# Moving three ScalarE, GpSimd and VectorE steps within a batch round of a cross-attention and routed feed-forward kernel

## The reference

```python
# attention with 8 heads of 64 channels; q = layernorm(x), k = v = context
ig, fg = gates(concat(q, k, v))                       # 8 rows of 512 each
csum   = cumsum(log_sigmoid(fg))
log_D  = where(tril, csum_i - csum_j + ig_j, -inf)
D      = exp(log_D - max(log_D))                      # the decay
C      = (q @ k.T / 8 + q . rpe[hops]) * D
h      = C / (max(abs(sum(C)), exp(-max_log_D)) + 1e-6) @ v
x      = x + layernorm_per_head(h) * (1 + ln_w) + ln_b
# feed-forward: a dense layer, and a mixture of the best two of 10 experts (2 of them null), rank 16
y      = layernorm(x)
w      = top2(softmax(y @ gate_w.T))
x      = x + y @ base_w.T + base_b + 2 * sum_e w_e * (y @ A_e.T) @ B_e.T
```

## Time and profile before

| | us |
|---|---|
| median of 3 runs (4051.57 to 4079.62) | 4066.55 |
| the profiled execution's own time | 4108.5 |
| its span, first to last instruction | 4106.8 |
| PE busy | 3321.3 (81%) |
| DVE busy | 2492.5 (61%) |
| POOL busy | 2075.7 (51%) |
| ACT busy | 1915.9 (47%) |

### The profile page before, as it was taken

One profiled execution on the slowest core, in us unless ns is written; L12 is line 12 of the kernel. 1 busy time (PEld: TensorE's weight loads), 2 busy tenths in 40 slices (PEclk: granted clock), 3 DMA queues, 4 the chain that ended last, 5 costly groups with the idle time before them and its releaser, 6 DMA issues.

```text
span 4106.8 us, 70340 instructions
## 1 busy us (share of the span) xinstructions
PE 3321.3 (81%) x24884; PEld 2008.6 (49%) x24884; DVE 2492.5 (61%) x5113; ACT 1915.9 (47%) x4609; POOL 2075.7 (51%) x2248
## 2 busy tenths in 40 slices
PE   5665667767667766666799999999999999999998
PEld 3433434434444434443455555555555555555554
DVE  4333433334433443434688887878788787878885
ACT  1323323323333333333566566666656565566654
POOL 4555455554555555554345454544545454545544
PEclk7788888787888888888899999999999999999999
DMA  6777777777787778787555555555545555555542
GB/s 195 249 233 223 247 235 225 246 244 233 247 253 249 247 246 258 246 260 238 169 164 174 161 166 161 171 163 166 168 154 173 156 166 156 167 159 176 161 139 83
DMA packets 409680, 814.15 MB, mean 198 GB/s; under 512 B 100314, under 2 KB 204762, under 8 KB 407284
## 3 DMA queue, kind: packets, MB, share of 16 engines
q1 hardware_dynamic: 303860, 453.05, 35.4%
q0 software_dynamic: 87040, 285.28, 23.3%
q10 hardware_dynamic: 18432, 71.31, 4.6%
HBM read 632.67 MB, written 176.69 MB: 197 GB/s over the span
## 4 chain that ended last, share of the span: by engine, by line
PE 52%; DVE 12%; issue 8%; another core or an unknown queue 7%; DMA 6%; SPq 6%; POOL 5%; ACT 5%; ACTq 0%; POOLq 0%; DVEq 0%
PE psum L1445 15%; PE psum L1461 10%; SPq L562 5%; PE psum L1558 5%; PE psum L1528 5%; PE psum L1607 4%; PE psum L1540 4%; DMA arena<-gate_rows 3%; PE psum L1472 3%; PE psum L1611 2%; PE psum L1415 2%; DMA gate_rows<-arena 2%; DVE arena L498 2%; PE psum L1587 2%
## 5 line engine op out<-in xcount | busy, mean ns | idle before, releaser
L674 POOL DMA_INDIRECT arena<-in_L_xattn_rpe_dram,arena x768 | 730.1, 951 | 559.1 <-PE psum L1445 251.8
L1445 PE MATMUL psum<-arena 128*128 128x128 f32 x4352 | 744.9, 322 | 271.4 <-DVE arena L489 89.0
L1445 PEld LDWEIGHTS psum<-arena 128*128 128x128 f32 x4352 | 579.3, 165 | 562.6 <-issue 425.5
L498 DVE COPY arena<-psum 128x416 f32<-128x416 f32 (+15 forms) x512 | 224.1, 441 | 831.7 <-remote 356.4
L1461 PE MATMUL psum<-arena 64*32 64x416 f32 (+7 forms) x8192 | 513.1, 480 | 232.8 <-ACT arena L489 70.7
L498 ACT COPY arena<-psum 128x416 f32<-128x416 f32 (+15 forms) x512 | 199.3, 390 | 888.7 <-remote 361.4
L857 ACT ACTIVATE arena<-arena 128x512 f32<-128x512 f32 (+3 forms) x1024 | 497.7, 557 | 143.2 <-DMA arena<-gate_rows 103.3
L1607 PE MATMUL psum<-arena 128*128 128x512 f32 x1024 | 497.0, 599 | 23.2 <-DVE arena L1158 21.6
L1198 DVE TENSOR_TENSOR arena<-psum,arena 128x1024 f32<-128x1024 f32 (+1 forms) x384 | 387.2, 1043 | 152.1 <-PE psum L1540 147.0
L665 POOL DMA_INDIRECT arena<-in_L_xattn_rpe_dram,arena x320 | 302.7, 946 | 331.7 <-PE psum L1445 207.7
L693 POOL TENSOR_SCALAR_AFFINE_SELECT arena<-arena 128x256 f32<-128x256 f32 x256 | 139.8, 546 | 493.9 <-ACT arena L857 492.8
(11 more groups left out here) (106 smaller groups left out, 4879.5 us busy)
## 6 DMA issues: line engine op xcount, KB each, us to landing
arena<-in_x_dram SPq DMA_DIRECT2D x256, 256.0 KB, 4.3
arena<-gate_rows SPq DMA_DIRECT2D x128, 512.0 KB, 4.5
arena<-in_x_dram SPq DMA_DIRECT2D x512, 64.0 KB
arena<-in_ctx_dram SPq DMA_DIRECT2D x32, 1024.0 KB, 7.5
out_dram<-arena SPq DMA_DIRECT2D x128, 256.0 KB, 2.0
arena<-in_L_xattn_rpe_dram,arena POOLq DMA_INDIRECT x1088
arena<-hop_products SPq DMA_DIRECT2D x128, 128.0 KB, 2.6
arena<-hop_products SPq DMA_DIRECT2D x128, 120.0 KB, 2.5
```

The costliest lines, as they stand in the source:

```text
L498: copy(hop_out[c][:, lo:lo + width], bank(3 + 2 * (v % 2) + i, width)).then_inc(*line.inc(o))
L674: nc.gpsimd.indirect_dma_start(out=rows[v][:, t, :], out_offset=None, in_=rpe[:, :], in_offset=bass.IndirectOffsetOnAxis(ap=here[:, t, v:v ...
L1445: last = nc.tensor.transpose(turn_bank(o)[:, q * P:(q + 1) * P], own[:, q * P:(q + 1) * P], ident)
```

## The change

Four steps change places in three engines' lists; no instruction is added or removed.

```diff
 # POOL
                 if rf:
                     with_bias(rf, 0)
+                    scale(rf, 1)
                 if rp:
                     center(1)
-                if rf:
-                    scale(rf, 1)
-                if rp:
                     center(2)
                 if ra:
                     masks(ra, 3)
 # ACT
                 if rf:
                     ffn_norm(rf, 1)
+                if ra:
+                    unit_decay(ra, 8)
                 if rp:
                     gate_log()
-                if ra:
-                    unit_decay(ra, 8)
                 if rf:
                     mix_turned(rf, 0)
...
                 if rf:
                     ffn_norm(rf, 3)
-                if rp:
-                    unit_decay(rp, 0)
                 if rf:
                     mix_turned(rf, 2)
                 if ra:
                     pair_out(ra, 2)
                 if rf:
                     ffn_turned(rf, 3)
                 if rn:
                     root(rn, 0)
                     root(rn, 1)
+                if rp:
+                    unit_decay(rp, 0)
 # DVE
                 if ra:
                     pair_sums(ra, 0)
+                if rf:
+                    layer(rf, 1)
                 if rp:
                     value_means(3)
-                if rf:
-                    layer(rf, 1)
```

## The result

The changed kernel took 3967.34 us, median of 4 runs (3955.63 to 3978.38), against 4070.43 us, median of 4 runs of the kernel before. (Four steps moved; the "three" of the title are the engines.) The ratio is 0.9752, with a 95% interval of 0.9706 to 0.9799: faster by 2.5%. Forecast were 3977 us and a range of 3944 to 4024.

The account below looks back on a forecast made before the run. PE was taken to set the pace; 108 us of stalls and clock less 4.5 gave 103.5, a profiled execution of about 4005. With 14 us put down to the profiled run, gain 90, time 3977 us, range 3944 to 4024.

Parts of the forecast that it names:

- The ceiling: Over the 30 rounds, three PE stalls (51.6, 23.5, 26.4 us) and the clock's falls (6.7): at most 108 us to win.
- Step 1: On ACT, unit 0's decay goes last: the whole end-of-round stall, 51.6 us, and the clock's falls, 6.7, go.
- Step 2: On ACT, unit 8's decay goes ahead of gate_log: L908 moves up by 0.9 us; 0 to 50 with Step 3.
- Step 3: On POOL and DVE, the router starts 1.3 us earlier: "zi" stall, 26.4 us, goes; with Step 2, nearly all of 23.5.
- What is late next: On PE, gate_stats (L1513) begins to wait in rounds with the longest stalls: 0.15 us a round, 4.5 us off.
- From profile to median: Of the profiled execution's 42 us over the median, a third, 14 us, was put in the end-of-round stall.
- that rival: DVE's chain from router to gate_stats stretches when POOL works; only 58 us stay, so 4008 us; chance 0.14.
- The wait did not move on: Rival: gate rows land later against PE, or gate_stats waits 1 to 2 us a round; 35 us left, 4031; chance 0.09.
- The slower case: Rival: layer(rf, 1) blocks DVE until POOL's three operations end, value_means(3) queued behind; 41 us slower or more, chance 0.03.

Follow-up runs that it names:

- decay0_only_b: Kernel before with only unit_decay(rp, 0) moved to the end of ACT's list: stretch 1956.6 us against 2016.5, ratio 0.9860.
- the pair: Kernel before with only scale(rf, 1) ahead of center(1) and layer(rf, 1) ahead of value_means(3): stretch 1980.8 us against 2016.5.
- decay10_behind: Whole change without DVE's move, and unit_decay(ra, 10) on ACT behind mix_turned(rf, 1) and ffn_turned(rf, 2): stretch 1904.6 us, median 3958.52, ratio 0.9717.
- dve_only: Kernel before with only DVE's layer(rf, 1) ahead of value_means(3): stretch 2045.3 us against 2016.5, 28.8 us longer.

## Why the prediction was right, point by point

- **The ceiling.** 108 us from rows of the trace before, less 4.5: 103.5. The rounds' stretch fell by 109.7 us, the medians by 103.1. Of the 109.7, 105.3 lie in the 29 full rounds, 3.63 us a round; 108 in 30 rounds is 3.60. Adding 0.16 us to each shown stall was right: the shown idle and the clock alone would have given 94. Term by term, the table has 49.8, 22.5, 26.5 and 6.8 us before and 0.0, 0.5, 0.2 and 0 after.
- **Step 1**, decay of unit 0: 58 forecast, 59.9 measured alone. Shown by decay0_only_b: only the end-of-round stall and the falls of the clock went. Its place was right: it starts 2.64 us behind L906 (forecast 2.9), without a wait, and ACT is idle 0.88 us behind it (forecast 0.5).
- **Step 2**, decay of unit 8: L908 of tile 0 came earlier, and its stall fell from 22.5 to 6.6 us with this move alone. That the total of 22.1 met the 20 expected was partly luck: 5.3 us came back at the copy of tile 1, and 13.5 were won at the end of the round and at the clock, which a second execution might not show.
- **Step 3**, POOL and DVE: the relief of both stalls came, but the split between the moves was wrong and the sum for the pair, 35.7 against 37 expected, partly luck. I held that each needs the other. POOL's move alone gives 55.5, DVE's costs 28.8 alone and 20 beside POOL's. The step that failed is "`value_means(3)`, 0.9 us, falls behind it: the router starts 2.2 - 0.9 = 1.3 us earlier", where I took L1293's 1.5 us for fixed. It is 0.68 when no `center` runs. The router's gain was 0.70 us in the pair and 1.67 with the whole change (L1291 2.30 us earlier; forecast 2.2), as L1151 lost or won its race. Against a stall of 0.88 us the 1.67 had room; 0.70 would have left a rest.
- **The parts don't add up**: 59.9 + 22.1 + 35.7 = 117.7 against 109.7. The executions of steps 2 and 3 contain 23.6 us won at the end of the round and at the clock, which step 1's 59.9 has in full already. Without them the two leave 35.1 us in the table, and the whole change took 45.5 from the same places, as its router is earlier.
- **What is late next.** I took off 0.15 us a round for `gate_stats`. In the full rounds it waits no longer than before: 4.5 us too many. What comes next is L906 of tile 1, 2.8 us in 29 rounds: in the round shown ACT starts it at 3085.08, behind a decay, and PE goes on at 3085.53. In decay10_behind, with that decay behind it, the 2.8 us are gone.
- **From profile to median.** I put 14 us of the profiled run's 42 above the median into the end-of-round stall. Only one execution of the kernel before was profiled, so this isn't settled. The six other kernels that keep the stall had 4 to 13.5 us less of it and of the clock's falls, so some of the 14 may have been there; and the kernel after reached its first `gate_stats` 40.6 us earlier in its profiled run than the kernel before, on unchanged code, so the larger part may lie ahead of the rounds. Without this term the forecast is 4066.55 - 103.5 = 3963, against 3967 measured; with it, 3977, 10 us off.
- **The rivals.** DVE did lose time to POOL (1.14 us at L1277, which took 0.93 before, and 1.35 at L1291, 1.50 before), as that rival has it. It cost PE nothing, since the router had gained 1.7 us (it starts 13.16 us behind L1470's wait for L827, at 3067.68, and started 14.83 behind it before). In the pair it did cost: 0.9 and 0.6 us at L1151, which the forecast doesn't name. The wait did not move on. The slower case did not occur; dve_only is the nearest to it, 28.8 us, by that mechanism: the means behind a wait for POOL.

## What to carry to other kernels

Look for the stall of the engine that sets the pace, follow it to the instruction its releaser sat on, and ask whether that one has a reader as urgent as the one behind it; here the operation that waited for a round trip through memory belonged at the end of its engine's list, behind everything that was ready. Measure a change in one phase by two landmarks of that phase in the trace, not by the span: here the span's difference was 40 us too large. Add up each wait over that phase too, also the part too short to be shown: two of the part kernels met their expected total by what another stall happened to lose. And try the parts of a change alone: one of these four moves was of no use and hid how good another was.

## What the runs showed of the hardware

- A DVE operation with two SBUF inputs, of one element a partition, that started with 0.2 us or more of a POOL tensor operation still to run ended 0.01 to 0.02 us behind it, in all 33 such cases of the kernel before's rounds (L1279); the line takes up to 1287 ns instead of 160. One with an input in PSUM took 0.22 us beside POOL. The same computation with a pointer scalar took at most 216 ns and made the kernel before 27 us faster in its rounds, 21 of them by "zi".
- A `tensor_scalar` of 8 elements on DVE took 0.17 us when its start is shown 24 ns or more ahead of a POOL operation's, and mostly 1.08 when it was closer; where the rest of the order was the same, the router then stood at 14.15 instead of 13.17 us.
- The first `gate_stats` came at 1931 to 1975 us in ten profiled runs and at 1475 to 1486 in four on one chip. The rounds' stretch of the whole change repeats within 0.4 us (1906.8 and 1907.2), while the end-of-round stall and the clock's falls of the kernels that keep them range from 43 to 57 us.
- Filling 0.35 us of PE idle with other matmuls gave 0.29 us a round at that place, and the next copy that PE waits for took most of it back: the shortest round fell by 0.09.
